# Where the running sums of an attention kernel are turned, and where its products for maxima stand

## The reference

```python
x = x + L0_xattn(_layernorm(x), ctx, mask, ...)   # softmax over 12544 keys, with a mask
x = x + L0_attn(_layernorm(x), ...)               # causal linear attention and a GELU MLP
x = x + L0_ffn(_layernorm(x), ...)                # ternary weights, 8-bit activations
x = x + L1_xattn(_layernorm(x), ctx, ctx, ...)    # softmax over the same 12544 keys, no mask
x = x + L1_attn(_layernorm(x), ...)               # a decayed scan over time
x = x + L1_ffn(_layernorm(x), ...)                # ternary weights, a short convolution
```

## Time and profile before

| | |
|---|---|
| median of 3 runs | 1051.52 us (1050.48 to 1053.42) |
| profiled execution, its own time | 1048.49 us |
| its span, first to last instruction | 1046.8 us |
| mean granted TensorE clock | 0.995 |
| busy: TensorE, VectorE, ScalarE, GpSimd | 1000.7, 738.7, 679.5, 428.0 us |

### The profile page before, as it was taken

How to read it: one execution, slowest core, us unless ns; L and a number is a source line. 1 busy time by engine, 2 the same in 40 slices (tenths; PEclk the granted TensorE clock), 3 DMA queues, 4 the chain that set the end, 5 groups by cost and what they waited for, 6 DMA issues and landing times.

```text
span 1046.8 us, 30801 instructions
## 1 busy us (share of the span) xinstructions
PE 1000.7 (96%) x12905; PEld 679.2 (65%) x12905; DVE 738.7 (71%) x1731; ACT 679.5 (65%) x963; POOL 428.0 (41%) x388
## 2 busy tenths in 40 slices
PE   8899999999999999999877899999999999999987
PEld 5466666666666666665554566667666666766665
DVE  5788888888888888876457766555666556556476
ACT  2777877777787877877443556566556566565642
POOL 4369888898888888882000000101000001000011
PEclk9999999999999999999998999999999999999999
DMA  8520122111220122113022010111101111000000
GB/s 318 143 72 20 54 72 72 50 38 59 72 73 21 53 72 72 55 33 130 11 89 103 2 37 2 37 37 37 37 2 37 37 37 36 2 3 2 3 1 6
DMA packets 14683, 53.31 MB, mean 51 GB/s; under 512 B 3025, under 2 KB 4817, under 8 KB 13649
## 3 DMA queue, kind: packets, MB, share of 16 engines
q1 hardware_dynamic: 14544, 51.35, 14.3%
HBM read 51.21 MB, written 0.13 MB: 49 GB/s over the span
## 4 chain that ended last, share of the span: by engine, by line
PE 86%; DVE 9%; ACT 3%; issue 2%; DMA 0%; DVEq 0%; ACTq 0%
PE ps_out L1290 18%; PE ps_proj L1211 15%; PE ps_scores L1274 15%; PE ps_proj L1201 13%; PE ps_max L1218 9%; PE ps_scores L1270 4%; PE ps_scores L1201 3%; PE ps_proj L1301 2%; DVE tile_max L888 1%; DVE unread L885 1%; PE ps_proj L1191 1%; PE ps_scores L1211 1%; ACT probs L647 1%; PE ps_scores L1307 0%; DVE tile_max L897 0%
## 5 line engine op out<-in xcount | busy, mean ns | idle before, releaser
L888 DVE TENSOR_REDUCE tile_max<-ps_max 128x1 f32<-128x448 f32 x353 | 208.2, 619 | 146.4 <-PE ps_max L1218 142.1
L885 DVE CUSTOM_DVE_ANT_0 unread<-ps_max,masks 128x448 bf16<-128x448 f32 x372 | 218.3, 621 | 71.1 <-PE ps_max L1218 70.9
L494 POOL TENSOR_TENSOR probs<-probs,masks 128x512 f32<-128x512 f32 x182 | 228.0, 1275 | 67.5 <-ACT probs L635 65.9
L647 ACT ACTIVATE probs<-ps_scores 128x1024 f32<-128x1024 f32 x193 | 187.2, 1021 | 84.4 <-PE ps_scores L1274 84.3
L642 ACT ACTIVATE probs<-probs 128x1024 f32<-128x1024 f32 x196 | 207.2, 1057 | 49.3 <-DVE probs L946 42.8
L1274 PE MATMUL ps_scores<-q_pad,k_full 32*128 32x256 f32 x3088 | 232.6, 377 | 0.0
L1290 PE MATMUL ps_out<-probs,values 128*32 128x128 f32 x6272 | 213.8, 276 | 0.7 <-ACT probs L647 0.4
L1274 PEld LDWEIGHTS ps_scores<-q_pad,k_full 32*128 32x128 f32 x3088 | 194.2, 186 | 0.6
L1290 PEld LDWEIGHTS ps_out<-probs,values 128*32 128x32 f32 x6272 | 158.6, 109 | 51.6 <-issue 47.0
L1218 PE MATMUL ps_max<-k_high,q_high 32*128 32x448 bf16 x729 | 174.0, 357 | 8.4 <-DVE tile_max L888 5.5
L1211 PE MATMUL ps_proj<-ctx_t,wk 128*128 128x448 f32 x384 | 169.4, 563 | 1.7
(11 more groups left out here) (270 smaller groups left out, 921.0 us busy)
## 6 DMA issues: line engine op xcount, KB each, us to landing
ctx_t<-in_ctx_t SPq DMA_DIRECT2D x28, 896.0 KB, 5.2
masks<-in_mask_n SPq DMA_DIRECT2D x14, 448.0 KB, 3.4
masks<-in_mask_t SPq DMA_DIRECT2D x14, 448.0 KB, 3.5
room_w<-in_L_attn_f_w SPq DMA_DIRECT2D x2, 1024.0 KB, 8.2
room_w<-in_L_ffn_w SPq DMA_DIRECT2D x2, 1024.0 KB, 8.3
room_w<-in_L_ffn_w_gate SPq DMA_DIRECT2D x1, 1024.0 KB, 10.5
room_w<-in_L_ffn_w_up SPq DMA_DIRECT2D x1, 1024.0 KB, 12.8
room_w<-in_L_ffn_w_down SPq DMA_DIRECT2D x1, 1024.0 KB, 14.8
```

What stands on the lines that cost most here:

```text
L494: nc.gpsimd.tensor_tensor(p, p, three(mask_t[m % 2], TILES)[:, t, :].unsqueeze(1).to_broadcast([P, 4, P]), ALU.add).then_inc(sig("bias_add ...
L647: nc.scalar.activation(prob(T, half), scores_half(T, half), ACT.Exp).then_inc(sig(f"exp_done{half}"), 1)
L885: ins = v.tensor_tensor_reduce(unread[:, j % 2, :], max_bank(m, j)[:, 0:HALF], mask_n[m % 2][:, HALF * half:HALF * (half + 1)], 1.0, -3e38 ...
L888: ins = v.tensor_reduce(tile_max[:, h, half:half + 1], max_bank(m, j)[:, 0:HALF], AX_X, ALU.max)
```

## The change

- `turn_sums` goes from between scores and weighing to behind the visit of the same tile, and from `ps_proj` to the lent score bank; the next tile's scores wait for `add_sums`. The last blocks (13 and 27) keep the old place. On VectorE `add_sums` goes behind the visit's maxima.
- In tile 1 of each block one product more stands beside the scores, in `ps_proj`. The two tables take the visit of tile 4 out of layer 1's blocks, and those of tiles 2 and 5 out of layer 2's.
- The product that sums the first three weight matrices goes from tile 0 to tile 1 of block 0. At the start, the last key copy on ScalarE goes behind the copy of the row of maxima.
- In block 13 the idle products have 128 columns instead of 256. Three idle products are added in tile 0 of block 14, and three near the end.
- GpSimd's last cast between the layers waits for VectorE's second layer norm there.

```diff
-        SCORED_AT = ((2, 0, 2, 1, 2, 1, 1), (2, 1, 2, 2, 2, 2, 2))
-        WEIGHED_AT = ((0, 2, 0, 2, 1, 2, 2), (0, 2, 1, 1, 0, 1, 0))
+        SCORED_AT = ((2, 1, 2, 1, 2, 1, 1), (2, 2, 2, 2, 2, 2, 2))
+        WEIGHED_AT = ((0, 2, 0, 2, 0, 2, 2), (0, 2, 0, 2, 0, 0, 0))
+        def sums_turned_in(m, t):
+            return in_stage(m, t) == SUMS_AT and stage(m, t) > STAGES_OF[m // NB][0]
         def late_bank(m, t):
-            return m < NB and t >= LAST_AT
+            return m < NB and (t >= LAST_AT or m > 0 and t == SUMS_AT)
...
-                        two = m > 0 and k == 0 and len(here) == 2 and in_stage(m, t) != SUMS_AT
+                        two = m > 0 and k == 0 and len(here) == 2
...
+                            if (k, c) == (NB + 1, 1):
+                                pool.wait_ge(sig("ln2_applied"), 1)
                             high(k, c)
...
-                    for u in range(4, len(FIRST)):
+                    for u in range(4, len(FIRST) - 1):
                         first_out(u)
...
                 rows_out(NB * l)
+                if l == 0:
+                    first_out(len(FIRST) - 1)
...
                         for k, j in behind_weighing:
                             maximum(k, j)
+                        if sums_turned_in(m, t) and not is_last(m):
+                            add_sums(stage(m, t) - 1, ps_scores[:, 0, :])
...
+                if t > 0 and sums_turned_in(m, t - 1) and not is_last(m):
+                    pe.wait_ge(sig("acc_added"), stage(m, t))
...
                         proj_free(None)
-                        idle_products(1, ps_proj)
+                        mm(ps_proj[:, 0:P], ident[:, :], ident[:, :], start=True, stop=True)
...
+                        if m == 0 and t == SUMS_AT:
+                            proj_free(("w_scaled", 1))
+                            pe.wait_ge(sig("abs_sums"), 3)
+                            mm(ps_proj[:, 0:3], ones[:, :], w_sum[:, 0:3], start=True, stop=True).then_inc(sig("w_sums"), 1)
+                        if sums_turned_in(m, t) and is_last(m):
                             proj_free(("acc_added", stage(m, t)))
                             turn_sums(stage(m, t) - 1)
...
+                        if sums_turned_in(m, t) and not is_last(m):
+                            turn_sums(stage(m, t) - 1, lent(m, t))
...
+                        if (m, t) == (NB, 0):
+                            idle_products(3)
...
-            idle_products(6)
+            idle_products(9)
```

More of the change, by code:

```diff
@@ L932, in late_ternary, with add_sums @@
                 v.tensor_scalar(tern[n][:, :], w, ROUND, None, ALU.subtract).then_inc(sig("late_ternary"), 1)
-            def add_sums(m):
+            def add_sums(m, bank=ps_proj):
                 dve.wait_ge(sig("acc_decayed"), m + 1)
                 dve.wait_ge(sig("sums_turned"), m + 1)
-                v.tensor_tensor(acc[:, :, :], acc[:, :, :], ps_proj[:, :].rearrange("p (h w) -> p h w", h=H)[:, :, 0:HD + 1],
+                v.tensor_tensor(acc[:, :, :], acc[:, :, :], bank[:, :].rearrange("p (h w) -> p h w", h=H)[:, :, 0:HD + 1],
                                 ALU.add).then_inc(sig("acc_added"), 1)
@@ L1004, in _ @@
                             maximum(k, j)
-                        if in_stage(m, t) == SUMS_AT and stage(m, t) > STAGES_OF[l][0]:
+                        if m == 0 and t == SUMS_AT:
+                            weight_scales(ps_proj[:, 0:3], slice(0, 3), "w_sums")
+                        if sums_turned_in(m, t) and is_last(m):
                             add_sums(stage(m, t) - 1)
@@ L1020, in _ @@
                             chain(chained(m, t))
-                        if m == 0 and t == 0:
-                            weight_scales(ps_proj[:, 0:3], slice(0, 3), "w_sums")
                 add_sums(STAGES_OF[l][1] - 1)
@@ L1282, in weigh @@
                     pe.wait_ge(sig("v_copied"), PAIRS * m + PAIRS)
+                    if m == 0:
+                        pe.wait_ge(sig("k_copied"), 8)
                 if in_stage(m, t) == 0:
@@ L1294, in weigh, with turn_sums @@
                         proj_free(None)
-                        idle_products(1, ps_proj)
+                        mm(ps_proj[:, 0:P], ident[:, :], ident[:, :], start=True, stop=True)
                 last.then_inc(sig("pv_done"), 1)
-            def turn_sums(m):
+            def turn_sums(m, bank=ps_proj):
                 pe.wait_ge(sig("sums_copied"), m + 1)
                 for c in range(4):
-                    last = tr(ps_proj[:, P * c:P * (c + 1)], out_t[:, P * c:P * (c + 1)], ident[:, :])
+                    last = tr(bank[:, P * c:P * (c + 1)], out_t[:, P * c:P * (c + 1)], ident[:, :])
                 last.then_inc(sig("sums_turned"), 1)
@@ L1416, in _ @@
                 if l == 0:
-                    pe.wait_ge(sig("k_copied"), 8)
+                    pe.wait_ge(sig("k_copied"), 7)
                 for n in range(NB):
@@ L1438, in _ @@
                         projections(m, t)
-                        if m == 0 and t == 0:
-                            proj_free(("w_scaled", 1))
-                            pe.wait_ge(sig("abs_sums"), 3)
-                            mm(ps_proj[:, 0:3], ones[:, :], w_sum[:, 0:3], start=True, stop=True).then_inc(sig("w_sums"), 1)
+                        if (m, t) == (NB, 0):
+                            idle_products(3)
                         for k, j in ahead:
```

## The result

The changed kernel takes 1046.39 us (median of 6 runs, 1046.10 to 1047.08) against 1050.37 for the kernel before on the same chip (6 runs, 1049.62 to 1053.42): ratio 0.9969, 95% interval 0.9958 to 0.9980. That is 4.0 us less. The forecast was 7.0 less, with 1039.5 to 1049.0 as its range. The sign was right, the size wrong; and the two steady parts came out with their signs exchanged.

What follows compares the result with a forecast made beforehand. TensorE, busy 96% of the span, was taken as the bound. The terms (-4.3 + 1.2 - 0.7 - 1.0 - 0.6 - 0.6 - 0.8 - 0.2) sum to -7.0 us, from the median 1051.52 to 1044.5; range 1039.5 to 1049.0.

Steps and rivals of the forecast that it cites:

- Layer 2: Blocks 16 to 26: dropped visits save 0.28 in tile 2, 0.11 in tile 5, tile 1 zero; 4.3 us less (3.1 to 6.2).
- The turn: Tile 1 of layer 2: turning the sums takes 0.58 us in either place, so moving it changes nothing.
- Rival 2: Gains more: turn a tenth cheaper (0.06 each), clock holds, layer 1 level; 11.0 less, 1040.5 us; chance 0.17.
- Layer 1: Blocks 1 to 12: tile 1 costs 0.38, tile 4's dropped visit gives 0.28; 1.2 us more (3.4 less to 4.6 more).
- Start: Block 0: first scores 0.3 earlier by swapped copies, 0.4 of a 0.9 wait gained; 0.7 us less (0 to 1.2).
- Block 13: Five idle products cut to 128 columns give about 0.2 each; 1.0 us less (0 to 1.0).
- Between the layers: GpSimd's cast no longer lies over VectorE's L1061 (1.03 against 0.43); 0.6 us less (0 to 0.6).
- Blocks 14 and 15: Three moved turns give 0.2 each, 0.6 us less; three idle products in block 14 keep the clock, 0.8 less.
- Tail: Three more idle products near the end keep the clock for some twenty small products; 0.2 us less (0 to 0.4).
- Rival 3: Gets slower: the addition of the sums is late behind the visit's maxima, next scores wait; 3.2 us slower; chance 0.06.
- Rival 1: Hardly gains: layer 1 waits grow, tile 4 gives nothing (+4.6); 1.8 less, 1049.7 us; chance 0.15.

Runs made afterwards that it cites:

- Experiment 2: Changed kernel with layer 2's two products beside the scores, where a visit follows, taking their banks in the other order (ps_max first, then ps_proj): 1038.38 us, 0.9883 against before.
- experiment 3: Changed kernel with layer 2's two tables put back to those before, so there only the turn of the sums has moved: 1043.15 us, 0.9941 against before.
- experiment 6: Changed kernel with layer 1's two tables put back to those before, so there only the turn of the sums has moved: 1049.41 us, one run.
- experiment 8: Experiment 2 with VectorE's copy of the means at the start written as a reciprocal of the scales: 1035.49 us, 0.9867 against before.
- experiment 1: Changed kernel with the product summing the weights, and VectorE's three steps on it, back in tile 0 of block 0: 1046.63 us, 0.9965 against before.
- experiment 5: Experiment 2 with block 0's start as before: sums in tile 0, key copies ahead of the row, wait for all eight: 1035.26 us, 0.9865 against before.
- experiment 7: Experiment 5 with one idle product instead of three in the first tile of block 14: 1035.00 us, 0.9863 against before.
- experiment 4: Changed kernel without the three idle products in the first tile of block 14: 1047.87 us, 0.9985 against before.
- experiment 9: Experiment 8 with layer 1's turn back beside the scores, its displaced product in tile 3, both products read ahead of VectorE's bias: 1038.13 us, 0.9881 against before.
- experiment 10: Experiment 9 with the second product's maximum in tile 3 of layer 1 read behind VectorE's bias addition: 1051.87 us, 1.0016 against before.
- experiment 11: Experiment 9 with the other order of the banks in layer 1 too (ps_max first, then ps_proj): 1039.03 us, 0.9903 against before.

## Why the prediction was right and wrong

- **Layer 2 (forecast -4.3, measured +1.0): the step that failed.** I wrote that a visit costs 0.28 and that the moved product goes beside another "for the price of one". The price on TensorE is right: tiles 2 and 5 gave 0.47 together (forecast 0.39). But I priced a product and not its bank. Filling the pair of tile 1 and the visit of tile 3 to two products each put VectorE's last read of ps_max behind the moment at which the visit wants it: 0.40 and 0.29 us a block. I counted VectorE's reads only up to the addition of the sums, and there they are indeed in time. Experiment 2 removes that wait alone and gives 8.0, of which 7.5 lie in these blocks; with it blocks 16 to 26 are 6.5 shorter than before, beyond even the forecast's upper bound of 6.2.
- **The turn (forecast 0 in layer 2): 0.19 cheaper behind the visit** (experiment 3). I had taken 0.58 at either place. The Trainium skill, TensorEngine Tiling (Array Packing), Key Properties, says that a change of tiling mode drains the array, and by it the turn next to a projection should cost less: the trace agrees in direction, at three times the 0.06 that the second rival allowed. That the drain is the cause is argued, not shown: no run sets the mode change apart from the rest of the move.
- **Layer 1 (forecast +1.2, measured -1.3): two terms mis-sized.** Tile 1 cost 0.31 (forecast 0.38). The visit taken from tile 4 gave 0.43 and not 0.28: the missing 0.15 is the wait of the products ahead for VectorE's read (228.66 above), the same kind of wait for a bank that I left out in layer 2, here on the gaining side. Tile 2 gave 0.07 and tile 5 took 0.09. The mechanism in tile 1 was half right: it is the exponentials that set it, but they set it with or without the product (experiment 6), so what costs is the turn.
- **Start (forecast -0.7, measured +0.3, and up to +1.9): wrong.** The first scores did come 0.30 earlier. Of the 0.9 of wait I assumed 0.4 as gain; the new wait of the values is 1.88, of which 0.8 is the copy that stands still under GpSimd's addition (experiment 8); and the key copies, put behind the row, make the sums wait 1.40 in tile 0 (experiment 1). The prediction had neither.
- **Block 13 (forecast -1.0, measured -0.4):** four tiles fell from 2.97 to 2.82, 0.15 each and not 0.2; one of the four took 3.01, and 2.82 in experiments 2 and 8. The fifth idle product is in the last tile, where the 0.21 it gives is gone again by the next weighing.
- **Between the layers (-0.6): -0.62,** by the mechanism stated.
- **Blocks 14 and 15 (forecast -1.4, measured -2.1):** right in kind. The three moved turns gave 0.34, 0.41 and 0.37 in their tiles and not 0.2 each. What is left, 1.0, goes to the clock (forecast 0.8), which fell once there and not twice; the idle products' own 0.10 is in it. That size is in part luck: the same code with no fall at all takes 1.4 less (experiment 6).
- **Tail (-0.2): nothing, though the clock held.** Before, it is at 0.50 from about 1029.5 to 1033.0, just where sixteen small products stand; with nine idle products no profile shows a fall there. TensorE and VectorE, before and after:

```profile
1029.30 1.74 PE L1554 MATMUL ps_scores<-xn_t,tern 128*128 128x128 bf16 x16 [0.35 <-ACT xn_t L787]
1030.29 1.48 DVE L1154 TENSOR_TENSOR masks<-ps_scores,probs 128x512 f32<-128x512 f32 x2 [0.95 <-PE ps_scores L1554]
```

```profile
1027.25 1.07 PE L1572 MATMUL ps_scores<-xn_t,tern 128*128 128x128 bf16 x16 [0.35 <-ACT xn_t L795]
1028.33 1.29 DVE L1164 TENSOR_TENSOR masks<-ps_scores,probs 128x512 f32<-128x512 f32 x2 [1.03 <-PE ps_scores L1572]
```

  The products take 1.07 instead of 1.74, yet VectorE starts 1.08 behind their first and not 0.99. Before, it starts when the eighth is done, as it is told to; after, only when the sixteenth is. In experiments 1, 5 and 7, which have the sums of the weights in tile 0, it starts behind the eighth again, and the tail is 49.46 to 49.49 instead of 49.8. So the idle products are worth 0.3 there, and moving the sums takes it back; by what way, no run shows.
- **Rival 3** (the addition is late) is excluded by the rows: the addition ends 1.12 us ahead of the next scores in layer 2 and 0.69 in layer 1, where 0.8 or more was worked out; only block 14's turn is open. **Rival 2's** part on the turn held, and layer 1 did come out level or better. **Rival 1's** number (1.8 less) is nearer to what was measured than the forecast's 7.0, but its mechanism fell: the dropped visit of layer 1 gave more than forecast, not nothing.

The sum of the misses is 3.8 us: 5.3 too little in layer 2, 1.0 at the start, 0.6 in block 13 and 0.2 in the tail, against 2.5 more than forecast in layer 1 and 0.7 in blocks 14 and 15. The range held mainly by that exchange, which is luck and not foresight.

**What stays open** is how often the clock falls. Up to block 14 experiments 2, 3, 4 and 6 are the changed kernel's code, save for 6's layer 1. In three of these five profiles the clock is at 0.50 for about 3 us soon after the wait of 1.88, which makes block 0 1.6 us longer (39.72 to 39.75); in the other two it isn't. With the wait of 1.07 (experiments 8 to 11), or with the sums in tile 0 (before, and 1, 5 and 7), it didn't fall there once. Six executions of the changed kernel lie within 1.0 us, but ten of experiment 1 are spread over 6.2; some of the spread of every kernel here is likely such falls, in block 0, between the layers (experiments 2, 3, 10 and 11, where that stretch takes 68.0 to 68.5 instead of 67.4) and in block 14. No run fixed that cause alone.

## What to carry to other kernels

A product has two prices: its time on the engine that makes it, and the time at which its bank is read. Before a group is filled up, write down for each bank the last reader ahead of the next writer; where two banks are read in a row, the one that is wanted first must be read first. And an operation that stands in another engine's shadow is nearly free there: moved out of it, it costs time again (0.31 us a tile here), however good the new place is.

## What the runs showed of the hardware

- A VectorE copy of 128x3 from SBUF to SBUF took 0.99 us under a GpSimd addition and ended with it (0.17 elsewhere), while a reciprocal of the same size in the same place took 0.18. VectorE additions of two SBUF tensors were stretched from 0.43 to 1.03 under GpSimd's cast, before and after, each time whichever of them started inside it. The Trainium skill, SBUF — State Buffer, SBUF: two separate sides, says that of a GpSimd operation and a VectorE operation in a two-port mode, or with two SBUF inputs where GpSimd's reads SBUF, the one that starts first has the shared ports for its whole instruction and the other stands still. The trace agrees for the copy and the additions; the reciprocal wasn't held.
- The same four transposes cost 0.19 us less a tile between products and a full-array projection than between scores and weighing (tile 1 of layer 2, 5.00 against 5.19).
- TensorE's granted clock fell to 0.50 (1.2 GHz) behind a wait of 1.88 us in block 0 in three of five profiles of nearly the same code, and behind a wait of 1.07 in none of four.
- In block 14, ten profiles with three idle products show one fall in nine (32.05 to 32.22 us) and none in one (30.66); of the two profiles without them one shows two falls (33.41) and the other a fall of 17 us (35.90). TensorE was at work most of the time around each fall.
